# Last token products behind batch 1's u, batch 2's low part on GpSimd, interleaved combination, values ahead of transposes for four tiles

## The reference

```
xn   = (x - mean) / sqrt(var + 1e-5)                 # per token
q, k, v = xn Wq^T + bq, xn Wk^T + bk, xn Wv^T + bv
qk   = q k^T                                         # 1024 x 1024 per batch
th   = 0.5 + 0.2 sigmoid(qk) + 0.15 tanh(qk) + 0.1 relu(qk)
s    = (softmax(th) v) Wo^T + bo
e    = argmax(softmax(xn Wr + br))                   # one expert per token
y    = gelu(xn W1[e] + b1[e]) W2[e] + b2[e]
out  = x + s * silu(y)
```

## Time and profile before

| what | value |
|---|---|
| median of 3 runs | 574.48 us |
| the profiled execution | 574.2 us, its span 572.5 us |
| PE busy | 543.8 us (95%), weight loads 511.1 us (89%) |
| DVE, ACT, POOL busy | 408.8 us (71%), 338.1 us (59%), 196.0 us (34%) |
| chain that ended last | PE 65%, DVE 15%, ACT 6%, issue 6%, POOL 5% |
| DMA | 56.88 MB, mean 99 GB/s |

### The profile page before, as it was taken

One profiled execution on the slowest core, in us unless ns is written; L12 is line 12 of the kernel. 1 busy time (PEld: TensorE's weight loads), 2 busy tenths in 40 slices (PEclk: granted clock), 3 DMA queues, 4 the chain that ended last, 5 costly groups with the idle time before them and its releaser, 6 DMA issues.

```text
span 572.5 us, 11249 instructions
## 1 busy us (share of the span) xinstructions
PE 543.8 (95%) x3987; PEld 511.1 (89%) x3988; DVE 408.8 (71%) x804; ACT 338.1 (59%) x608; POOL 196.0 (34%) x230
## 2 busy tenths in 40 slices
PE   4999999899999999999999998999699999999996
PEld 3878898788999999999999998998599988999995
DVE  6787588934847765478555686476699998777895
ACT  3377778525536644355443554385777878777882
POOL 3126338911322112221112211005994444323553
PEclk9999999979999999999999998999899999999999
DMA  8823920015421551115511211005432111111111
GB/s 285 306 92 130 342 82 1 1 50 228 139 100 47 193 202 37 46 55 192 201 37 37 55 57 38 18 18 175 129 128 77 56 51 53 37 56 56 57 55 56
DMA packets 40306, 56.88 MB, mean 99 GB/s; under 512 B 3607, under 2 KB 35358, under 8 KB 39726
## 3 DMA queue, kind: packets, MB, share of 16 engines
q1 hardware_dynamic: 35276, 45.89, 23.4%
q0 software_dynamic: 3488, 9.47, 5.5%
q10 hardware_dynamic: 1506, 1.06, 0.6%
HBM read 40.68 MB, written 17.56 MB: 102 GB/s over the span
## 4 chain that ended last, share of the span: by engine, by line
PE 65%; DVE 15%; ACT 6%; issue 6%; POOL 5%; ACTq 2%; DMA 1%; DVEq 0%; SPq 0%; POOLq 0%
PE ps L782 20%; PE ps L784 19%; PE ps L783 19%; POOL token_at L458 5%; PE ps L877 4%; DVE hidT_h L1488 2%; DVE theta L1231 2%; DVE hidT_l L1490 1%; PE ps L937 1%; DVE theta L1235 1%; ACT hid L689 1%; DMA xn_all<-in_L_attn_x_dram 1%; DVE stats L1177 1%; ACT tanh_s L581 1%; PE ps L1046 1%
## 5 line engine op out<-in xcount | busy, mean ns | idle before, releaser
L689 ACT ACTIVATE hid<-ps,b_now 128x256 f32<-128x256 f32 x160 | 65.9, 472 | 30.1 <-PE ps L784 21.3
L782 PE MATMUL ps<-v_hi,pT_hi 128*128 128x258 f32 x256 | 76.0, 297 | 2.3 <-DVE pT_lo L1249 1.0
L783 PE MATMUL ps<-v_lo,pT_hi 128*128 128x258 f32 x256 | 72.4, 283 | 0.0
L784 PE MATMUL ps<-v_hi,pT_lo 128*128 128x258 f32 x256 | 72.2, 282 | 0.0
L1231 DVE SCALAR_TENSOR_TENSOR theta<-tanh_s,theta 128x512 f32<-128x512 f32 x64 | 50.3, 787 | 27.1 <-ACT tanh_s L581 26.3
L782 PE MATMUL ps<-w_hi_even,hidT_h 128*128 128x256 f32 x224 | 65.2, 291 | 0.5
L697 ACT ACTIVATE g_sb<-y_sb 128x512 f32<-128x512 f32 x20 | 12.6, 632 | 89.5 <-DVE y_sb L1495 89.5
L782 PE MATMUL ps<-rowT_h,w_hi_even 128*128 128x256 f32 x224 | 63.7, 284 | 1.2 <-issue 1.2
L783 PE MATMUL ps<-rowT_l,w_hi_even 128*128 128x256 f32 x224 | 63.4, 283 | 0.0
L784 PE MATMUL ps<-rowT_h,w_lo_even 128*128 128x256 f32 x224 | 63.4, 283 | 0.0
L784 PE MATMUL ps<-w_hi_even,hidT_l 128*128 128x256 f32 x224 | 63.4, 283 | 0.0
(11 more groups left out here) (218 smaller groups left out, 1693.9 us busy)
## 6 DMA issues: line engine op xcount, KB each, us to landing
w_raw_odd<-in_L_ffn_W_dram SPq DMA_DIRECT2D x10, 1024.0 KB, 7.3
w_raw_even<-in_L_ffn_W_dram SPq DMA_DIRECT2D x6, 1024.0 KB, 6.3
sorted_g<-g_sb SPq DMA_DIRECT2D x20, 256.0 KB, 2.1
xn_rows<-xn_all SPq DMA_DIRECT2D x4, 1024.0 KB, 6.0
x_tile<-in_L_attn_x_dram SPq DMA_DIRECT2D x32, 128.0 KB, 2.2
out_dram<-g_tile SPq DMA_DIRECT2D x32, 128.0 KB, 1.7
xn_all<-in_L_attn_x_dram SPq DMA_DIRECT2D x3, 1024.0 KB, 12.2
kept_xT<-passing_xT SPq DMA_DIRECT2D x2, 1024.0 KB, 4.2
```

The costliest lines, as they stand in the source:

```text
L689: last = nc.scalar.activation(hid[:, j % 2, c * UNIT:(c + 1) * UNIT], ps[:, HID_BANK + j, c * UNIT:(c + 1) * UNIT], ACT.Gelu, bias=b1_now[ ...
L782: mm(dst, a_hi, b_hi, start=first, stop=False)
L783: mm(dst, a_hi, b_lo, start=False, stop=False)
L784: return mm(dst, a_lo, b_hi, start=False, stop=last)
```

## The change

Four things are changed.

1. **Token products.** The last eight `invert`s stood between the u products of batch 1 (q = 0 and 1). They now stand behind all four. VectorE makes all four `low_u(1, q)` before it copies the token list.
2. **Start of the last expert.** `low_xT(2)` moves from VectorE to GpSimd, behind its loop of row gathers. ScalarE and VectorE no longer read the last expert's unit numbers there: `last_unit` is read one expert earlier, and the first number is the one that is known from the expert before (u1).
3. **Combination.** `COMBINED` was 0 to 5, 8, 6, 9, 7, 10, ...; it is now 8, 9, 10, 0, 11, 1, 12, 2, ... 18, 19, ...
4. **Tiles 9 to 13.** In tile 10 `weighted(n - 1)` stood ahead of `transposes(n)`; now it does in tiles 10 to 13, with VectorE's order to match (`finish` and `transposed_parts` between the two halves of `thetas`). On ScalarE `transposed_high(9)` goes between the halves of `acts(10)`, and `high_u(2, 0)` ahead of `exps(10)`.

```
+        VALUES_FIRST = range(TPB + 2, TPB + 6)
...
-        COMBINED = list(range(6)) + [8, 6, 9, 7] + list(range(10, NT))
+        COMBINED = [TPB, TPB + 1, TPB + 2]
+        for n in range(TPB):
+            COMBINED += [n, TPB + 3 + n]
+        COMBINED += list(range(2 * TPB + 3, NT))
...  GpSimd, behind the loop of row gathers
+            for k in range(DC):
+                pool.wait_ge(lnT_hi, 4 + DC + k + 1)
+                nc.gpsimd.tensor_tensor(xnT_lo[place_of_batch(2)][:, k, :], own_xT[:, k, :],
+                                        xnT_hi[place_of_batch(2)][:, k, :].bitcast(F32), ALU.subtract
+                                        ).then_inc(lnT_lo, 1)
...  ScalarE, last two experts
             u0, u1 = units_of(E - 2)
+            last_u = act.value_load(last_unit[0:1, 0:1], min_val=E - 1, max_val=MAX_UNITS - 1)
             pick_b1(E - 2)
             first_unit_of(u0, 1, E // 2 + 1)
             other_units(u0, u1)
-            u0, u1 = units_of(E - 1)
-            last_u = act.value_load(last_unit[0:1, 0:1], min_val=E - 1, max_val=MAX_UNITS - 1)
             high_xT(2)
             pick_b1(E - 1)
-            with act.If(u0 < last_u):
-                with act.Fori(u0, last_u) as u:
+            with act.If(u1 < last_u):
+                with act.Fori(u1, last_u) as u:
                     unit(u)
...  ScalarE, tiles
-                    for h in range(2):
-                        acts(n + 1, h)
-                    if n > TPB:
+                    job = next_job(n)
+                    acts(n + 1, 0)
+                    if n == TPB + 1:
                         transposed_high(n)
-                    exps(n + 1)
-                    job = next_job(n)
+                    acts(n + 1, 1)
+                    if n > TPB + 1:
+                        transposed_high(n)
+                        exps(n + 1)
                     if job:
                         (high_u if job[0] == "u" else high_v)(*job[1:])
+                    if n <= TPB + 1:
+                        exps(n + 1)
...  TensorE, batch 1's u
-                first = 3 * TPB + 4 * q
-                u_product(1, q, inverted=[[first + 2 * k, first + 2 * k + 1] for k in range(DC)] if q < 2 else ())
+                u_product(1, q)
+            for t in range(3 * TPB, NT):
+                invert(t)
...  TensorE, tiles
-            scores(TPB + 3)
-            weighted(TPB + 1)
-            transposes(TPB + 2)
-            job(TPB + 2)
-            for n in range(TPB + 3, NT - 1):
+            for n in range(TPB + 2, NT - 1):
                 if (n + 1) % TPB == 0:
                     pe.wait_ge(u_ready, (n + 1) // TPB * 4 + 4)
                 scores(n + 1)
-                pe.wait_ge(pT_ready, n * 2)
+                if n in VALUES_FIRST:
+                    weighted(n - 1)
+                else:
+                    pe.wait_ge(pT_ready, n * 2)
                 transposes(n)
                 if next_job(n):
                     job(n)
-                weighted(n - 1)
+                if n not in VALUES_FIRST:
+                    weighted(n - 1)
...  VectorE, last two experts
-            u0, u1 = units_of(E - 1)
-            last_u = dve.value_load(last_unit[0:1, 0:1], min_val=E - 1, max_val=MAX_UNITS - 1)
             dve.wait_ge(b2_in, 16 * E)
-            low_xT(2)
...  VectorE, tiles
+            for n in range(TPB + 2, NT - 2):
+                if n in VALUES_FIRST:
+                    thetas(n + 1, [0])
+                    finish(n - 1)
+                    transposed_parts(n)
+                    dve.wait_ge(mixed, (n + 1) * 3 + 2)
+                    thetas(n + 1, [1])
+                    job(n)
+                else:
+                    thetas(n + 1)
+                    transposed_parts(n)
+                    job(n)
+                    finish(n - 1)
```

More of the change, by code:

```diff
@@ L824, in offset_products, with u_product @@
                 bias_product(7, KEY_COL, wq_raw, BK).then_inc(offsets_done, 1)
-            def u_product(b, q, routed=(), inverted=()):
+            def u_product(b, q, routed=()):
                 m, h, bank = u_job(b, q)
@@ L844, in u_product @@
                         turn_0(2 + k)
-                    for t in inverted[k] if inverted else ():
-                        invert(t)
             def v_product(b, q, routed_batch=None):
@@ L1464, in _ @@
             finish(6)
-            for q in range(2):
+            for q in range(4):
                 low_u(1, q)
@@ L1469, in _ @@
             v.tensor_copy(sorted_token[:, :], ps[:, 7, 0:COLUMNS]).then_inc(tokens_ready, 1)
-            for q in range(2, 4):
-                low_u(1, q)
             finish(TPB - 1)
@@ L1545, in _ @@
             u0, u1 = units_of(E - 2)
+            last_u = dve.value_load(last_unit[0:1, 0:1], min_val=E - 1, max_val=MAX_UNITS - 1)
             first_unit_of(u0, E - 2, 0)
             other_units(u0, u1, 0)
-            u0, u1 = units_of(E - 1)
-            last_u = dve.value_load(last_unit[0:1, 0:1], min_val=E - 1, max_val=MAX_UNITS - 1)
             dve.wait_ge(b2_in, 16 * E)
-            low_xT(2)
-            with dve.If(u0 < last_u):
-                with dve.Fori(u0, last_u) as u:
+            with dve.If(u1 < last_u):
+                with dve.Fori(u1, last_u) as u:
                     unit(u, 1)
@@ L1577, in _ @@
             job(TPB + 1)
-            thetas(TPB + 3, [0])
-            finish(TPB + 1)
-            transposed_parts(TPB + 2)
-            dve.wait_ge(mixed, (TPB + 3) * 3 + 2)
-            thetas(TPB + 3, [1])
-            job(TPB + 2)
-            for n in range(TPB + 3, NT - 2):
-                thetas(n + 1)
-                transposed_parts(n)
-                job(n)
-                finish(n - 1)
+            for n in range(TPB + 2, NT - 2):
[11 more added lines that the diff above has]
+                    finish(n - 1)
             thetas(NT - 1, [0])
```

## The result

The changed kernel takes 567.77 us, the median of 4 runs (567.54 to 571.24), against 575.05 us of the kernel before beside it (4 runs, 574.42 to 575.72). The ratio is 0.989, with a 95% interval of 0.987 to 0.992. The profiled execution took 567.67 us, its span is 565.9. Forecast were 567.1, from 561.0 to 570.5.

What follows compares the result with a forecast made beforehand. TensorE, busy nearly the whole span, was taken to bind, its waits costing themselves plus half-speed clock behind them. From the profiled 574.2 us, -6.2 (A) - 1.8 (B) + 0.9 (C) = -7.1 gave 567.1 us, range 561.0 to 570.5.

Steps and rivals of the forecast that it cites:

- A: Token products in batch 1's u: TensorE's wait for `token_at` (2.6 us) and slow clock (3.6) go, 6.2 us gained.
- the margin: First expert's gathered rows: they still land ahead of TensorE's need, with 2.5 us left of 5.7.
- B: Start of the last expert: moved load and low part bring `y_sb` earlier, 1.8 us gained; bounds 3.4 gained, 0.7 lost.
- GpSimd's 4.8 us: Last expert: `low_xT(2)` as two GpSimd subtractions, 4.8 us behind its last row gather, at no cost.
- C: Tiles 9 to 14: 1.7 us gained, 1.6 of slow clock and 1.0 of later waits paid, 0.9 us lost.
- the round: Tiles 10 to 13: one cycle from exponentials to next exponentials takes 9.0 us, 8.4 undisturbed, against TensorE's 7.92 per tile.
- The waits at jobs: Tiles 11 to 13: each job waits about 1 us for the low part of the job before it.
- the waits at tiles 14 and 17: A job of tile 14 and batch 3's first at tile 17 wait, ScalarE and VectorE lacking lead: 1.0 us together.
- Rival 1: Tiles 11 to 14: exponentials come early enough, all waits there and half the slow stretch go, 560.1 us; chance 0.19.
- the ring: Tiles 10 to 13: exps, hi of u, tanh, thetas, finish, parts, thetas, next exps; slower than TensorE even undisturbed.
- Rival 3: Tiles 10 to 13: theta operations each wait for a whole GpSimd operation, 12.2 us rounds, 576.7 us; chance 0.05.

Runs made afterwards that it cites:

- e3: Kernel before with only the new order of tiles 9 to 14 and of the combination: 575.32 us, ratio 1.002.
- e2: Kernel before with only batch 2's low part on GpSimd and the last expert's unit-number loads moved: 574.83 us, ratio 0.998.
- e8: Changed kernel with batch 2's low part back on VectorE, the loads still moved: 569.28 us, ratio to before 0.990.
- e12: Changed kernel with the unit numbers read where the kernel before reads them, low part still on GpSimd: 576.29 us, ratio to before 1.004.
- e6: Changed kernel with batch 0's tiles combined between tiles 17 to 24 instead of 11 to 18: 567.61 us, ratio to before 0.985.
- e1: Kernel before with only the last eight token products behind all four u quarters and the token list copied later: 570.63 us, ratio 0.993.
- e4: Changed kernel with values ahead of transposes in tile 10 alone: 563.97 us, ratio to before 0.981.
- e11: Changed kernel with batch 0 combined between tiles 17 to 24 and transposes ahead of values in tile 10 too: 562.13 us, ratio to before 0.977.
- e10: Kernel before with the new order of the combination alone: 573.66 us, ratio 0.9969.
- e5: Changed kernel with the old order of the combination: 572.29 us, ratio to before 0.995.
- e7: Changed kernel with values ahead of transposes in tile 10 alone and batch 0 combined between tiles 17 to 24: 564.96 us, ratio to before 0.983.
- e9: Changed kernel with values ahead of transposes in tiles 10 to 15 instead of 10 to 13: 573.08 us, ratio to before 0.996.

## Why the prediction was right, and where it wasn't

**A: right, 5.8 instead of 6.2 us.** No wait, clock 1.00, 6.4 us between the two products. The term that was mis-sized is the eight token products: they take 0.81 us in a row, not 0.5. The 0.13 us for two was read from the earlier trace rows as the distance to the next product's start; that product then takes 0.21 us to the one behind it, where other products of 258 columns take 0.12, so the pair costs 0.22 us, 0.11 for each, there as well. The other 0.1 us are the 24 u products, 5.6 us (110.85 to 116.45) for 5.5. The gather was issued at 120.04, against 120.4 forecast, and the margin held. What the prediction took as certain was the slow clock of the kernel before, 3.6 of its 6.2 us. e3 shows the same wait with the clock up, and there the place costs 9.4 us: A is worth 5.8 us where the clock falls, and 3.0 where it doesn't.

**B: right in size, wrong in one cause.** -1.8 us at `y_sb` (e2), a wait of 0.27 (0.25 forecast). But the loads alone make it: with the low part back on VectorE the wait stays as short (e8). Their price was misread on the way: the 2.12 us between the starts of the gate and of `high_xT(2)` hold the gate itself, which is followed after 0.54 us in the changed kernel, so three loads take 1.6 us and not 2.1. The load that was moved ahead of the gate delays it by 0.65 us (339.49 against 338.84 in e12), for 0.7 forecast. The prediction gave GpSimd's 4.8 us no cost, because nothing waits for the result. That holds by margins of 1.6 us ahead of it and 0.6 behind it; where it meets a cast, it costs 4.7 us (e12). The prediction looked for who waits for GpSimd, not for who runs beside it.

**C: right in kind, 1.2 us lost instead of 0.9.** Transposes of tile 9 come 7.77 us earlier than before, those of tile 14 8.72, those of tile 20 only 6.56: C has won 0.95 us by tile 14 (1.7 forecast) and lost 1.2 by tile 20. The term that was mis-sized is the round, 9.27 and not 9.0 us, three times. The undisturbed round was 8.47 against 8.4 forecast (e6), so GpSimd's part is 0.8 and not 0.6. The longest wait and its slow stretch came at `transposes(14)` as said, 2.90 us and 1.7. The waits at jobs were two, 0.7 and 0.8 us, instead of three of about 1. Part of the match is luck: the rounds took 0.75 us more of the gain than forecast, and the waits at tiles 14 and 17, put at 1.0 us, were 0.5, all of it at tile 17.

**The sum.** -5.8 - 1.9 + 1.2 = -6.5 us, against -6.6 of the two spans; forecast -7.1. The 0.6 between are 0.4 of A and 0.3 of C, less 0.1 of B. This sum goes by places in one trace, not by edits that were taken back. The medians of the parts alone, -4.1, +0.1 and +0.6 us, come to -3.4 and not to the -7.3 of all three. Of the difference the profiles of e1 and e2 show 0.9 to 1.0 us each in the tiles and 1.5 each of clock behind tile 31. A and B together without C was never run; next to the tile stretches of e1 and e2 (179.0 and 179.1 without the clock) the changed kernel's 179.3 is hardly longer, so what C costs on top of A and B may be less than 1.2.

**Rival 1** (the ring doesn't bind) was wrong for the changed kernel, but e4 and e11 show what it had in view: without the ring in tiles 11 to 13 the kernel comes down to 564 and 562 us. Part C was several edits with different signs. The new combination alone wins 0.95 us (e10), the old one in the changed kernel loses 1.4, mostly by `finish` waiting for GpSimd (e5), and values ahead of transposes in tiles 11 to 13 costs 3.1 us of tile stretch without the clock (e4 against the changed kernel), 4.8 with it. ScalarE's new order was not tried by itself.

**Rival 3** (full blocking) is both wrong and right. The three theta operations of the earlier trace rows grew by 0.3 to 0.4 us each beside GpSimd operations that take 0.74 us alone and grew too:

```profile
404.08 1.23 POOL L498 TENSOR_TENSOR g_tile<-half,g_tile 128x256 f32<-128x256 f32 x1
405.38 1.07 POOL L501 TENSOR_TENSOR g_tile<-g_tile,x_tile 128x256 f32<-128x256 f32 x1
...
408.43 1.14 POOL L501 TENSOR_TENSOR g_tile<-g_tile,x_tile 128x256 f32<-128x256 f32 x1
```

The one of 1.55 us in the changed kernel grew by 0.80 us, about the length of one GpSimd operation, so that alone doesn't speak against full blocking; that GpSimd's second operation grew beside it, 0.74 to 1.08, fits. By the Trainium skill (page "SBUF — State Buffer", section "Who interferes with whom") the loser stands still for the whole of the other's operation. The trace of before disagrees for the three operations of the earlier trace rows, and that of e12 agrees for the cast: 5.15 us instead of 0.42.

**Open.** A's and B's gains are each cut by 0.9 to 1.0 us in tiles 9 to 12 (e1, e2), with one more wait of 0.7 us for a low part of u. In the kernel before that wait falls into the half-clock stretch, which begins earlier there; that this is the whole cause wasn't tried.

## What to carry to other kernels

A wait of the bounding engine has two prices, its length and the clock behind it. The first is certain and the second isn't, so a forecast should give both numbers. An order of work that closes a ring through several engines should be timed as a round against the bounding engine's own time per tile, and kept for as few tiles as it is needed. Work that is moved to GpSimd "for free" needs two checks: who waits for it, and which VectorE operations run beside it; the one here that lost several us was a cast. And parts that are measured one at a time need not add up to the whole.

## What the runs showed of the hardware

- **The clock's fall is not settled by the program.** TensorE fell to half clock behind the token wait of 2.6 us in the profiles of before, e2 and e10, and not in e3; behind the hidden rows' wait of 1.8 to 1.9 in before, e3 and e10, not in e1 or e12 (in e12 it fell in the second wait, of 4.8 us); behind 1.8 us at tile 11 in e7 and not in e4. Of five waits of 2.0 to 2.3 us in the tiles, four were followed by a fall (two in e5, e10, e11) and one not (e6). Behind those of 2.87 us or more there it fell in all eight. In e1, e2 and e9 it fell behind the last waits of 0.5 and 1.0 us, where in the eleven others it held until TensorE was done. In e6, e8 and e9 it fell between 15 and 23 us, where in the eleven others it held on the same code. Each fall costs 1.5 to 1.7 or 3.4 us. The spread of single runs goes with it, 570.6 to 578.7 us for the kernel before, at mean granted clocks from 0.993 down to 0.978; four of e11's five runs lie between 561.6 and 562.2 at 1.0, the fifth at 563.9 with 0.996.
- **One VectorE cast stood still for two GpSimd operations in a row**, 5.15 us, and wasn't let in between them. It was seen once. It is the operation that takes 0.42 us for 128x512 elements; theta operations, which take 0.68 to 0.75, were drawn out by at most 0.8 in all fourteen profiles.
